# The last block of a relational graph layer, multiplied in two halves with upper and lower parts in one stationary

## The chip, the cores and the metric

The kernel runs on one core of a Trainium2 chip. The metric is the device time in microseconds (us); the number shown is the median of three runs.

## What is computed

A relational graph layer with a residual and a layer norm. There are 6250 nodes with 256 features, 206250 edges sorted by destination, and 16 relations with a 256 x 256 weight each:

```python
transformed = jnp.einsum('ni,rio->rno', h, weight)
msg = transformed[rel_type, src] * norm
out = jax.ops.segment_sum(msg, dst, num_segments=h.shape[0])
x = _layernorm(x + out, axis=-1)
```

## The kernel before

The kernel sums first and multiplies afterwards. Nodes go in blocks of 128 (SB); there are 49 blocks (NB), and the last one has 106 nodes (LAST). A block has four parts (groups) of 32 nodes (GN). For each part, edges come in tiles of 128. GpSimd gathers the source rows of a tile with an indirect DMA (L557) into `rows`. VectorE makes the tile's spread matrix (L786): one column for each pair of node and relation in the tile's window, the edge's weight where it belongs. TensorE multiplies the rows by the spread into PSUM `ps_a` (L983); this adds, for each node and relation, the weighted source rows, and is called A. Each step has two k-halves of 128 features, and the trace shows four matmuls a step (float32, two each).

When a part has all its tiles, ScalarE copies A out of PSUM with rounding (L857, the upper part `a_hi`, float32r), and VectorE subtracts this from PSUM to get what is left (L752, the lower part `a_lo`). Upper and lower weights lie side by side in `w_parts`. The products of a block are 32 k-tiles (16 relations x 2 halves). For each, the upper A of 128 nodes is the stationary against upper and lower weights, 512 columns (L942), and the lower A is the stationary against the upper weights, 256 columns (L944). They add up in one bank of `ps_z`. `normalise` (L725 to L743) on VectorE adds the node's own row and both halves of the bank, makes mean and variance, waits for ScalarE's square root (L881), and writes the normalised rows, which SP stores (L522).

The order is written out by hand. Each engine runs through the same list of blocks and steps (`blocks`, L416), and the engines are held together by semaphores only. At step t of block b, TensorE does the sums of the step and then some products of block b-1, from step 8 on (`products_at`, L178). In the last block (39 steps, 0 to 38) these are two k-tiles a step at steps 8 to 23. After the last block come two rounds of 40 steps without sums: the first holds the products of the last block (from step 8 on, with nothing between), the second its normalisation. `normalise(b)` handles block b-2 and stands at step 10 (NORM_AT) of round b; block 47 is thus normalised in the round behind the sums.

Evacuation lags behind the sums: ScalarE copies a part 4 steps after it closes (EVAC_LAG), VectorE subtracts 9 steps after (LOWER_LAG), counted in each engine's own list. In the last block, part 192 (group 0) closes at step 11, part 193 at step 22, part 194 at step 33, part 195 (10 nodes) at step 38. So VectorE's subtractions for part 193 stand in its list at step 31, behind that step's spread. The spreads have 17 slots, so VectorE can be 17 steps ahead of TensorE. The spreads of steps 23 to 38 have 96, 160, 208, 208, 224, 224, 240, 192, 144, 80, 96, 96, 160, 128, 64 and 16 columns.

SP's list has, for each block, the edge loads, and then the wait for that block's normalisation, the store of its rows, and the load of the next own rows into `xr`. At the end it waits for the last normalisation, and stores 96 and 10 rows (L525 to L528).

Of the kernel before, what the change touches and what calls it, by code (L numbers as in the profile page):

```python
# [87 lines left out]
def build(nc, x, src, dst, rel, norm, weight, out):  # L88
# [86 lines left out]
    NORM_AT = 10  # L175
    ENDED_AT, TOTAL_STEP, FLAG_AT = 12, 14, 18

    def products_at(b, t):  # L178
        if b == NB - 1:
            return 2 if PRODUCT_FROM <= t < PRODUCT_FROM + KH * R // 2 else 0  # L180

        def upto(t):
            return 0 if t < PRODUCT_FROM else ceil(KH * R * (t - PRODUCT_FROM + 1) / (length[b] - PRODUCT_FROM))
        return upto(t) - upto(t - 1)
# [15 lines left out]
    with ExitStack() as ctx:  # L200
# [114 lines left out]
        def spread_at(n):  # L315
# [5 lines left out]
                return over_below[:, later * WMAX:later * WMAX + WMAX]  # L321
            return over_w_raw[:, (later - fit) * WMAX:(later - fit) * WMAX + WMAX]

        hit_cmp = z_rows.rearrange("p n f -> p (n f)")[:, 0:2 * SROW].rearrange("p (q e) -> p q e", q=2)

        ps_f = ps_m[:, 256:512]
# [55 lines left out]
        a_upper_made = sem("a_upper_made")  # L382
        products_made = sem("products_made")
        own_rows_in = sem("own_rows_in")
        residual_added = sem("residual_added")
        upper_added = sem("upper_added")
        variance_steps = sem("variance_steps")
# [37 lines left out]
        def prepared(b, t, step):  # L425

            if b == 0:
                return [1] if t == FIRST_PREPARE[step] else []
            found = [2] if b == 1 and t == SECOND_PREPARE[step] else []
            if t == PREPARE[step] and 3 <= b + AHEAD < NB:  # L430
                found.append(b + AHEAD)
            return found

        evacuated_at = {}
        for part, n in closes.items():
# [36 lines left out]
        def fast_sync(sp):  # L472
            def load_edges(b):

                for s in range(GROUPS):
                    n = GROUPS * (b - 1) + s
                    first = sp.value_load(first_i[0:1, n:n + 1], min_val=0, max_val=E)
                    sp.dma_start(raw[PT * s:PT * s + PT, :, :],
                                 packed[:, bass.ds(first, PART_EDGES)].rearrange("a (j p) -> j a p", p=P)).then_inc(
                                     edges_in, 16)  # L480

            def raw_left(b):

                sp.wait_ge(edges_converted, b)
                sp.wait_ge(edges_turned, b)

            def load_weights(n):
                if n >= 2:

                    sp.wait_ge(w_lower_made, n - 1)  # L490
                sp.dma_start(w_raw[:, n % 2, :, :], weight[n, :, :].rearrange("(k p) n -> p k n", p=P)).then_inc(
                    weights_in[n % 2], 16)

            sp.dma_start(direct_idx[:, :], src[0:DIRECT * P].rearrange("(j p) -> p j", p=P),
                         allow_slow_non_contiguous=True).then_inc(direct_idx_in, 16)
            for a, v in enumerate((src, dst, rel, norm_i)):
                sp.dma_start(raw[0:CT, a, :], v[0:CE].rearrange("(j p) -> j p", p=P)).then_inc(edges_in, 16)

            sp.dma_start(sample_i[0:SP, :], dst.rearrange("(p c e) -> p c e", c=SC, e=SROW)[:, :, 0],
                         allow_slow_non_contiguous=True).then_inc(samples_in, 16)  # L500
            sp.dma_start(xr[:, :], x[0:SB, :]).then_inc(own_rows_in, 16)
            for n in range(WEIGHTS_BEFORE):
                load_weights(n)

            sp.wait_ge(first_edges_ready, 1)
            sp.wait_ge(edges_packed, 8 * 16)
            raw_left(1)
            load_edges(1)
            for n in range(WEIGHTS_BEFORE, R):
                load_weights(n)  # L510
            raw_left(2)
            load_edges(2)
            raw_left(3)
            load_edges(3)
            for b in range(1, NB):
                if b + 3 < NB:
                    raw_left(b + 3)
                    load_edges(b + 3)

                sp.wait_ge(rows_normalised, b)  # L520
                rows_of = min(SB, N - b * SB)
                sp.dma_start(out[(b - 1) * SB:b * SB, :], z_out[:, :]).then_inc(rows_out, 16)  # L522
                sp.dma_start(xr[0:rows_of, :], x[b * SB:b * SB + rows_of, :]).then_inc(own_rows_in, 16)

            sp.wait_ge(rows_normalised, NB)  # L525
            EVEN = LAST // 16 * 16
            sp.dma_start(out[(NB - 1) * SB:N - LAST + EVEN, :], z_out[0:EVEN, :]).then_inc(rows_out, 16)
            sp.dma_start(out[N - LAST + EVEN:N, :], z_out[EVEN:LAST, :]).then_inc(rows_out, 16)  # L528
            flag = uncounted(sp)
            sp.wait_ge(rows_out, (NB + 1) * 16)  # L530
            return flag

        def fast_pool(pool):
# [78 lines left out]
        def fast_vector(dve):  # L612
# [112 lines left out]
            def normalise(b):  # L725
# [16 lines left out]
                dve.tensor_scalar(z_out[:, :], z[:, :], z_mv[:, 0:1], z_rstd[:, :],  # L742
                                  ALU.subtract, ALU.mult).then_inc(rows_normalised, 1)  # L743

            def lower_part(part):
                b, g = part // GROUPS, part % GROUPS
                for h in range(KH):

                    dve.wait_ge(a_upper_made, KH * part + h + 1)
                    nodes = min(GN, N - GN * part)  # L750
                    at_g = slice(g * GN, g * GN + nodes)
                    dve.tensor_tensor(a_lo[:, b % 2, h, :, at_g],  # L752
                                      ps_a[:, g % OPEN, h, 0:nodes * R].rearrange("p (n r) -> p r n", r=R),
                                      a_hi[:, b % 2, h, :, at_g].bitcast(F32), ALU.subtract).then_inc(
                                          a_lower_made, 1)

            def tile_block(b, sums, products, rows_):
                for t in range(length[b]):
# [30 lines left out]
                                          ALU.is_equal, ALU.mult).then_inc(spreads_made, 1)  # L789
                    for part in evacuated_at.get(n - LOWER_LAG, ()):  # L790
                        lower_part(part)
                    if rows_ and t == NORM_AT:
                        normalise(b)

            first_runs = runs([step.first * R for step in plan[0]])
            for base, t0, t1 in first_runs:
# [12 lines left out]
            seek_samples()  # L809
            seek = {SEEK_ROW: seek_row, SEEK_EDGE: seek_edge, SEEK_TABLE: seek_table, SEEK_COPY: seek_copy}  # L810
            blocks(dve, tile_block)


        def runs(values):
# [4 lines left out]
        def fast_scalar(act):  # L819
# [27 lines left out]
            def evacuate(part):  # L847
                b, g = part // GROUPS, part % GROUPS


                act.wait_ge(tiles_summed, signals(closes[part]))
                if g == 0:

                    wait(act, products_made, b, 1, -1)
                nodes = min(GN, N - GN * part)
                for h in range(KH):
                    act.activation(a_hi[:, b % 2, h, :, g * GN:g * GN + nodes],  # L857
                                   ps_a[:, g % OPEN, h, 0:nodes * R].rearrange("p (n r) -> p r n", r=R),
                                   ACT.Copy).then_inc(a_upper_made, 1)

            def tile_block(b, sums, products, rows_):
                for t in range(length[b]):
                    if sums:
                        if b == 0 and t in WEIGHTS_AT:
                            n = WEIGHTS_AT[t]

                            act.wait_ge(weights_in[n % 2], 16 * (n // 2 + 1))
                            act.activation(w_parts[:, n, :, 0, :], w_raw[:, n % 2, :, :], ACT.Copy).then_inc(
                                w_upper_made, 1)
                        for ahead in prepared(b, t, CONVERT):  # L870
                            convert_edges(ahead)
                        for ahead in prepared(b, t, COPY):
                            copy_edges(ahead)
                    for part in evacuated_at.get(start_of[b] + t - EVAC_LAG, ()):
                        evacuate(part)
                    if rows_ and t == NORM_AT:
                        if b == 2:

                            act.wait_ge(columns_made, 2)
                        wait(act, variance_steps, b, 2, -2)  # L880
                        act.activation(z_std[:, :], z_mv[:, 1:2], ACT.Sqrt, bias=eps_col[:, :]).then_inc(  # L881
                            deviation_made, 1)

            convert_edges(0)
            copy_edges(0)
            pack_edges()
            blocks(act, tile_block)

        def fast_tensor(pe):
            def seek_count():  # L890
# [38 lines left out]
            def product(b, n):  # L929
# [16 lines left out]
                if n == KH * R - 1:  # L946
                    ins.then_inc(products_made, 1)

            def tile_block(b, sums, products, rows_):
                done, arrived = 0, set()  # L950
                for t in range(length[b]):
                    if sums:
# [34 lines left out]
                                    start=opens[part] == n, stop=False, skip_group_check=True)  # L987
                        if n in ends:
                            ins.then_inc(tiles_summed, 1)
                    if products:  # L990
                        for _ in range(products_at(b, t)):
                            product(b, done)
                            done += 1


            pe.wait_ge(constants_made, 4)
# [216 lines left out]
```

## Time and profile before

| | |
|---|---|
| median of three runs | 2483.79 us (2480.95 to 2488.75) |
| span of the profiled execution | 2053.3 us |
| its own whole time | not given beside its span |
| TensorE (PE) busy | 1949.3 us, 95% |
| GpSimd (POOL) busy | 1536.3 us, 75% |
| VectorE (DVE) busy | 1264.7 us, 62% |
| ScalarE (ACT) busy | 272.9 us, 13% |
| mean granted clock of TensorE | 0.993 |

The span goes from the first to the last instruction of one profiled execution. PE is TensorE's matmul, PEld its weight load, which overlaps. Matmul ends are modelled: matmuls are pipelined, so the distance between two starts is what one costs, not its duration. The chain of waits follows the last instruction back to what released each step. PEclk is the clock granted to TensorE, 1.00 being 2.4 GHz and 0.50 being 1.2 GHz.

### The profile page before, as it was taken

The numbers are of one execution on the slowest core, as the hardware profiler recorded it, in microseconds if no ns is written. First come the engines' busy times: TensorE is split into PE (matmuls) and PEld (weight loads), VectorE is DVE, ScalarE is ACT, GpSimd is POOL, SyncE is SP. The second block draws the span as 40 slices with busy tenths as digits, with TensorE's granted clock in tenths as the row PEclk, the third lists the DMA queues.
The fourth block names the chain that finished last, engine by engine and source line by source line (L and its number), as shares of the span: only waits on it lengthen the run. The fifth ranks groups of instructions, "written<-read, shape, count | busy, mean of one in ns | idle before, by whom it ended". The sixth has DMA issues, their size and how long they took to land. (4 is left out here: it accounts for less than half of the span.)

```text
span 2053.3 us, 33711 instructions
## 1 busy us (share of the span) xinstructions
PE 1949.3 (95%) x11962; PEld 1813.6 (88%) x11962; DVE 1264.7 (62%) x3579; ACT 272.9 (13%) x557; POOL 1536.3 (75%) x1649
## 2 busy tenths in 40 slices
PE   5899999999999999999999999999999999999998
PEld 4799999998889888998898898888898889988887
DVE  5666666666666666666566656666665656566554
ACT  1211111111111111111111111111111111111110
POOL 7777777777777777777777777777777777777774
PEclk8999999999999999999999999999999999999999
DMA  6544334344444444434344434344433434444332
GB/s 205 150 113 118 114 113 118 114 113 113 118 114 113 113 118 113 114 113 118 113 114 113 117 113 114 112 115 116 114 113 113 119 113 113 113 117 114 112 111 76
DMA packets 107715, 239.00 MB, mean 116 GB/s; under 512 B 31226, under 2 KB 55642, under 8 KB 107482
## 3 DMA queue, kind: packets, MB, share of 16 engines
q0 software_dynamic: 77760, 212.43, 36.6%
q1 hardware_dynamic: 29342, 21.02, 3.5%
q10 hardware_dynamic: 440, 3.32, 0.4%
q8 instruction: 99, 1.62, 0.4%
q14 instruction: 74, 0.61, 0.1%
HBM read 230.23 MB, written 9.72 MB: 117 GB/s over the span
## 5 line engine op out<-in xcount | busy, mean ns | idle before, releaser
L557 POOL DMA_INDIRECT rows<-in_x,idx x1614 | 1528.1, 947 | 491.7 <-issue 330.6
L983 PE MATMUL ps_a<-spread,rows 128*128 128x96 f32 (+7 forms) x5700 | 1066.0, 320 | 61.3 <-DMA rows<-in_x,idx 33.3
L983 PEld LDWEIGHTS ps_a<-spread,rows 128*128 128x128 f32 x5700 | 877.8, 192 | 137.5 <-DVE spread L786 40.7
L942 PE MATMUL ps_z<-w_parts,a_hi 128*128 128x512 f32 x1568 | 803.9, 514 | 1.0 <-DVE a_lo L752 1.0
L752 DVE TENSOR_TENSOR a_lo<-ps_a,a_hi 128x512 fp32r<-128x512 f32 x392 | 251.2, 683 | 487.7 <-ACT a_hi L857 487.7
L786 DVE TENSOR_SCALAR spread<-ps_i,key,meta 128x96 f32<-128x96 f32 (+8 forms) x1415 | 542.4, 449 | 5.5 <-PE ps_a L983 5.5
L944 PE MATMUL ps_z<-w_parts,a_lo 128*128 128x256 f32 x1568 | 439.7, 280 | 0.0
L857 ACT ACTIVATE a_hi<-ps_a 128x512 fp32r<-128x512 f32 x392 | 212.3, 594 | 1230.8 <-PE ps_a L983 1230.8
L942 PEld LDWEIGHTS ps_z<-w_parts,a_hi 128*128 128x128 f32 x1568 | 298.7, 190 | 5.0 <-DVE a_lo L752 1.1
L944 PEld LDWEIGHTS ps_z<-w_parts,a_lo 128*128 128x128 f32 x1568 | 299.1, 191 | 1.8
L983 PE MATMUL ps_a<-w_raw,rows 128*128 128x208 f32 (+7 forms) x1452 | 273.8, 318 | 14.7 <-DMA rows<-in_x,idx 13.2
L983 PE MATMUL ps_a<-below,rows 128*128 128x224 f32 (+7 forms) x1452 | 274.1, 318 | 12.3 <-DMA rows<-in_x,idx 9.9
L983 PEld LDWEIGHTS ps_a<-w_raw,rows 128*128 128x128 f32 x1452 | 222.5, 190 | 34.9 <-DVE spread L786 11.2
L983 PEld LDWEIGHTS ps_a<-below,rows 128*128 128x128 f32 x1452 | 222.5, 190 | 32.7 <-DVE spread L786 9.8
L786 DVE TENSOR_SCALAR below<-ps_i,key,meta 128x96 f32<-128x96 f32 (+7 forms) x363 | 144.9, 448 | 0.0
L786 DVE TENSOR_SCALAR w_raw<-ps_i,key,meta 128x208 f32<-128x208 f32 (+7 forms) x363 | 144.7, 448 | 0.0
L702 DVE CAST idx<-meta 128x40 int32<-128x40 f32 x48 | 14.1, 294 | 203.5 <-ACT meta L835 203.5
L835 ACT ACTIVATE meta<-ps_m 128x160 f32<-128x160 f32 (+1 forms) x49 | 14.8, 303 | 375.9 <-PE ps_m L926 375.9
L720 DVE SCALAR_TENSOR_TENSOR key<-tile_no,tiles_of,key_all 128x10 f32<-128x10 f32 x192 | 44.3, 231 | 6.9
L881 ACT ACTIVATE z_std<-z_mv,eps_col 128x1 f32<-128x1 f32 x49 | 14.4, 295 | 132.8 <-DVE z_mv L736 132.8
L926 PEld LDWEIGHTS ps_m<-ident,raw_f 40*128 40x128 f32 (+1 forms) x147 | 13.0, 141 | 18.1 <-issue 17.1
L826 ACT ACTIVATE raw_f<-raw 40x384 f32<-40x384 int32 (+1 forms) x49 | 25.1, 512 | 7.2 <-DMA raw<-packed 4.8
(75 smaller groups left out, 263.5 us busy)
## 6 DMA issues: line engine op xcount, KB each, us to landing
rows<-in_x,idx POOLq DMA_INDIRECT x1614, 2.8
xr<-in_x SPq DMA_DIRECT2D x48, 128.0 KB
out<-z_rows SPq DMA_DIRECT2D x48, 128.0 KB
w_raw<-in_L_gnn_weight SPq DMA_DIRECT2D x16, 256.0 KB, 3.1
raw<-packed SPq DMA_DIRECT2D x192, 20.0 KB
packed<-in_src ACTq DMA_DIRECT2D x1, 805.7 KB, 6.0
packed<-in_dst ACTq DMA_DIRECT2D x1, 805.7 KB, 7.6
packed<-in_edge_type ACTq DMA_DIRECT2D x1, 805.7 KB, 9.1
```

What stands on the lines that cost most here:

```text
L557: pool.indirect_dma_start(rows[:, row, :], None, x, bass.IndirectOffsetOnAxis(ap=index, axis=0)).then_inc(arrived, 16)
L702: dve.tensor_copy(idx[:, k, :], m[:, 0, :]).then_inc(keys_made, 1)
L720: key_done(dve.scalar_tensor_tensor(out=key[:, k, PT * s:PT * s + PT], in0=tile_no[:, :], scalar=tiles_of[:, n:n + 1], in1=key_all[:, PT * ...
L752: dve.tensor_tensor(a_lo[:, b % 2, h, :, at_g], ps_a[:, g % OPEN, h, 0:nodes * R].rearrange("p (n r) -> p r n", r=R), a_hi[:, b % 2, h, :, ...
L786: dve.tensor_scalar(spread_at(n)[:, 0:width], iota[:, 0:width], key[:, b % SLOTS, step.column:step.column + 1], meta[:, b % SLOTS, 3, step ...
L826: act.activation(raw_f[0:C, :, :], raw[0:C, 0:3, :], ACT.Copy).then_inc(edges_converted, 1)
L835: act.activation(meta[:, k, :, 0:C], ps_m[:, 0:4 * C].rearrange("p (a t) -> p a t", a=4), ACT.Copy).then_inc(edges_copied, 1)
L857: act.activation(a_hi[:, b % 2, h, :, g * GN:g * GN + nodes], ps_a[:, g % OPEN, h, 0:nodes * R].rearrange("p (n r) -> p r n", r=R), ACT.Co ...
L881: act.activation(z_std[:, :], z_mv[:, 1:2], ACT.Sqrt, bias=eps_col[:, :]).then_inc(deviation_made, 1)
L942: pe.matmul(zk, a_hi[:, ak, h, r, :], w_parts[:, r, h, :, :].rearrange("p a f -> p (a f)"), start=n == 0, stop=False, skip_group_check=True)
L944: ins = pe.matmul(zk[:, 0:F], a_lo[:, ak, h, r, :], w_parts[:, r, h, 0, :], start=False, stop=n == KH * R - 1, skip_group_check=True)
L983: ins = pe.matmul(ps_a[:, g % OPEN, h, (begin - zero) * R:(stop - zero) * R], rows[:, step.row, h * P:(h + 1) * P], spread_at(n)[:, (begin ...
```

## The change

The last block's 106 nodes are multiplied in halves of 64 and 42 nodes. Groups 0 and 1 put their upper A into columns 0 to 63 and their lower A into columns 64 to 127 of the same `a_hi` buffer; groups 2 and 3 do the same in `a_lo`. One matmul of 512 columns a k-tile gives rows 0 to 63 (upper A by both weights) and rows 64 to 127 (lower A by both weights). The first half's products go in TensorE's list behind the sums of steps 27 to 37 of the last block, three a step; the second half's stand behind all sums. ScalarE copies the lower rows' first 256 columns down to the partitions of the upper rows, and VectorE adds own rows, both column halves and this copy before the statistics. Each half has its own store; the second half's own rows have a load of their own. The normalisation of block 47 moves to step 28 of the last block. The buffers are existing ones.

```diff
+    HALF_ROWS = (64, LAST - 64)
+    HALF_FROM, HALF_EACH, LAST_NORM_AT = 27, 3, 28
...
+        half_sum = (ps_z[:, (NB - 1) % 2, :], ps_m[:, :])
+        half_own = (xr, col_iota[:, 0:F])
...
+        def upper_at(part, h, nodes):
+            b, g = part // GROUPS, part % GROUPS
+            if b == NB - 1:
+                return (a_hi, a_lo)[g // 2][:, b % 2, h, :, GN * (g % 2):GN * (g % 2) + nodes]
+            return a_hi[:, b % 2, h, :, g * GN:g * GN + nodes]
+
+        def lower_at(part, h, nodes):
+            b, g = part // GROUPS, part % GROUPS
+            if b == NB - 1:
+                return (a_hi, a_lo)[g // 2][:, b % 2, h, :, 64 + GN * (g % 2):64 + GN * (g % 2) + nodes]
+            return a_lo[:, b % 2, h, :, g * GN:g * GN + nodes]
...
-            sp.wait_ge(rows_normalised, NB)
-            EVEN = LAST // 16 * 16
-            sp.dma_start(out[(NB - 1) * SB:N - LAST + EVEN, :], z_out[0:EVEN, :]).then_inc(rows_out, 16)
-            sp.dma_start(out[N - LAST + EVEN:N, :], z_out[EVEN:LAST, :]).then_inc(rows_out, 16)
+            sp.wait_ge(columns_made, 3)
+            late = N - HALF_ROWS[1]
+            sp.dma_start(half_own[1][0:HALF_ROWS[1], :], x[late:N, :]).then_inc(late_own_rows_in, 16)
+
+            sp.wait_ge(half_normalised, 1)
+            sp.dma_start(out[late - HALF_ROWS[0]:late, :], half_out[0][0:HALF_ROWS[0], :]).then_inc(rows_out, 16)
+            sp.wait_ge(half_normalised, 2)
+            EVEN = HALF_ROWS[1] // 16 * 16
+            sp.dma_start(out[late:late + EVEN, :], half_out[1][0:EVEN, :]).then_inc(rows_out, 16)
+            sp.dma_start(out[late + EVEN:N, :], half_out[1][EVEN:HALF_ROWS[1], :]).then_inc(rows_out, 16)
...
+            def normalise_half(n):
+                S, sums, step = slice(0, HALF_ROWS[n]), half_sum[n], count(6 * n + 1)
...
+                dve.wait_ge(half_products_made, n + 1)
+                dve.wait_ge(half_lower_moved, n + 1)
...
+                step_done(dve.tensor_tensor(half_one[n][S, :], half_own[n][S, :], sums[S, 0:F], ALU.add))
+                step_done(dve.tensor_tensor(half_two[n][S, :], half_one[n][S, :], sums[S, F:2 * F], ALU.add))
+                step_done(dve.tensor_tensor(half_one[n][S, :], half_two[n][S, :], half_low[n][S, :], ALU.add))
+                step_done(dve.bn_stats(z_stat[S, :], half_one[n][S, :]))
+                step_done(dve.bn_aggr(z_mv[S, :], z_stat[S, :]))
+                dve.wait_ge(half_deviation_made, n + 1)
+                step_done(dve.reciprocal(z_rstd[S, :], z_std[S, :]))
+                dve.tensor_scalar(half_out[n][S, :], half_one[n][S, :], z_mv[S, 0:1], z_rstd[S, :],
+                                  ALU.subtract, ALU.mult).then_inc(half_normalised, 1)
...
-                    if rows_ and t == NORM_AT:
+                    if rows_ and t == NORM_AT and b < NB:
                         normalise(b)
+                    if b == NB - 1 and t == LAST_NORM_AT:
+                        normalise(NB)
...
             blocks(dve, tile_block)
+            for n in range(2):
+                normalise_half(n)
...
+            def half_lower(n):
+
+                act.wait_ge(half_products_made, n + 1)
+                act.activation(half_low[n][0:HALF_ROWS[n], :], half_sum[n][64:64 + HALF_ROWS[n], 0:F],
+                               ACT.Copy).then_inc(half_lower_moved, 1)
...
+            def half_product(g, n):
+
+                r, h = n // KH, n % KH
+                if n == 0:
+                    pe.wait_ge(a_lower_made, (PARTS - GROUPS + 2 * g + 2) * KH)
+                    if g == 0:
+                        pe.wait_ge(residual_added, NB - 2)
+                    else:
+                        pe.wait_ge(flag_steps, 2)
+                        pe.wait_ge(edges_copied, NB)
+                ins = pe.matmul(half_sum[g], (a_hi, a_lo)[g][:, (NB - 1) % 2, h, r, :],
+                                w_parts[:, r, h, :, :].rearrange("p a f -> p (a f)"),
+                                start=n == 0, stop=n == KH * R - 1)
+                if n == KH * R - 1:
+                    ins.then_inc(half_products_made, 1)
...
-                    if products:
+                    if products and b < NB:
...
+                    if b == NB - 1 and t >= HALF_FROM:
+                        for n in range(HALF_EACH * (t - HALF_FROM), HALF_EACH * (t - HALF_FROM + 1)):
+                            if n < KH * R:
+                                half_product(0, n)
+                    if b == NB and t == 0:
+                        for n in range(KH * R):
+                            half_product(1, n)
```

ScalarE's step 10 for block 47 (the square root) moves to its step 28 in the same way, and after its list come, for each half, the copy and the square root.

## Rows read from the trace of the kernel before

**Rows 1.** The page: span, and TensorE's busy time.

```profile
span 2053.3 us, 33711 instructions
PE 1949.3 (95%) x11962; PEld 1813.6 (88%) x11962; DVE 1264.7 (62%) x3579; ACT 272.9 (13%) x557; POOL 1536.3 (75%) x1649
```

**Rows 2.** The gathers' line: duration ns min/median/max, first and last start; landing.

```profile
L557 POOL DMA_INDIRECT rows<-in_x,idx x1614: 942/946/1427, 8.5 to 2030.1; - x180
...
DMA to landing us min/median/max: 2.6/2.8/11.0
```

**Rows 3.** Waits over the span: us in total, times, longest.

```profile
PE ps_a L983 <- DMA rows<-in_x,idx: 56.4, 92, 1.6
```

**Rows 4.** Busy time in stretches (length, PE, PEld, DVE, ACT, POOL; clock; DMA).

```profile
2006.90:2026.96 20.06, 20.06 (x128) 18.63 (x128) 8.77 (x21) 2.17 (x4) 15.18 (x17) 1.00 0.41 114
2026.96:2035.50 8.54, 8.54 (x60) 8.39 (x59) 3.34 (x10) 1.09 (x2) 3.21 (x4) 1.00 0.31 75
2036.48:2048.06 11.58, 11.56 (x64) 9.80 (x64) 1.88 (x6) 0.29 (x1) 0.00 (x0) 1.00 0.07 22
```

**Rows 5.** Chain of waits in the last block: start, us, what.

```profile
2012.53 0.54 PE ps_a L983 x4
...
2015.17 0.70 PE ps_a L983 x4
...
2016.57 0.76 PE ps_a L983 x4
...
2023.93 0.27 PE ps_z L942
...
2026.96 8.55 PE ps_a L983 x60
```

**Rows 6.** Timeline of VectorE in the last block.

```profile
2014.52 1.36 DVE L786 TENSOR_SCALAR below<-ps_i,key,meta 128x224 f32<-128x224 f32 x3
2015.79 0.81 DVE L786 TENSOR_SCALAR w_raw<-ps_i,key,meta 128x192 f32<-128x192 f32 x2
2025.75 1.29 DVE L752 TENSOR_TENSOR a_lo<-ps_a,a_hi 128x512 fp32r<-128x512 f32 x2 [9.15 <-ACT a_hi L857]
...
2036.34 0.41 DVE L730 TENSOR_TENSOR z_rows<-xr,ps_z 128x256 f32<-128x256 f32 x1
```

**Rows 7.** Chain of waits behind the sums: start, us, what.

```profile
2036.48 0.50 PE ps_z L942
...
2037.10 0.23 PE ps_z L942
...
2047.93 0.13 PE ps_z L944
...
2048.09 0.43 DVE z_rows L730
...
2050.20 0.41 DVE z_rows L742
```

**Rows 8.** Timeline of SP: the last two stores.

```profile
2050.64 0.34 SPq L527 DMA_DIRECT2D out<-z_rows  x1
2051.03 0.36 SPq L528 DMA_DIRECT2D out<-z_rows  x1
```

**Rows 9.** Stretches around falls of the clock (columns as in rows 4).

```profile
57.89:60.15 2.26, 0.00 (x0) 0.00 (x0) 0.88 (x2) 0.63 (x1) 1.73 (x2) 1.00 0.76 250
...
63.47:66.98 3.51, 3.51 (x13) 3.47 (x14) 3.24 (x6) 0.63 (x1) 2.78 (x3) 0.50 0.74 232
...
2048.06:2050.10 2.04, 0.00 (x0) 0.00 (x0) 1.55 (x5) 0.29 (x1) 0.00 (x0) 1.00 0.00 0
2050.10:2053.30 3.20, 0.00 (x0) 0.00 (x0) 0.47 (x2) 0.00 (x0) 0.00 (x0) 0.50 0.13 37
```

**Rows 10.** ScalarE's evacuations from 2020 us on, by shape.

```profile
L857 ACT ACTIVATE a_hi<-ps_a 128x512 fp32r<-128x512 f32 x4 | 2.2, 595 | 20.4 <-PE ps_a L983 20.4
...
L857 ACT ACTIVATE a_hi<-ps_a 128x160 fp32r<-128x160 f32 x2 | 0.5, 302 | 1.2 <-PE ps_a L983 1.2
```

More of the change, by code:

```diff
@@ L176, in build @@
     ENDED_AT, TOTAL_STEP, FLAG_AT = 12, 14, 18
+    HALF_ROWS = (64, LAST - 64)
+    HALF_FROM, HALF_EACH, LAST_NORM_AT = 27, 3, 28
+    assert 64 == 2 * GN and NB % 2 and length[NB - 1] > HALF_FROM + KH * R // HALF_EACH
     def products_at(b, t):
@@ L322, in spread_at @@
             return over_w_raw[:, (later - fit) * WMAX:(later - fit) * WMAX + WMAX]
+        half_sum = (ps_z[:, (NB - 1) % 2, :], ps_m[:, :])
+        half_own = (xr, col_iota[:, 0:F])
+        half_low = (spread[:, 0, 0:F], spread[:, 1, 0:F])
+        half_one = (z_rows[:, 1, :], spread[:, 2, 0:F])
+        half_two = (z_rows[:, 0, :], spread[:, 3, 0:F])
+        half_out = (z_rows[:, 2, :], spread[:, 4, 0:F])
         hit_cmp = z_rows.rearrange("p n f -> p (n f)")[:, 0:2 * SROW].rearrange("p (q e) -> p q e", q=2)
@@ L384, in build @@
         own_rows_in = sem("own_rows_in")
+        late_own_rows_in = sem("late_own_rows_in")
+        half_products_made = sem("half_products_made")
+        half_lower_moved = sem("half_lower_moved")
+        half_steps = sem("half_steps")
+        half_deviation_made = sem("half_deviation_made")
+        half_normalised = sem("half_normalised")
         residual_added = sem("residual_added")
@@ L523, in fast_sync @@
                 sp.dma_start(xr[0:rows_of, :], x[b * SB:b * SB + rows_of, :]).then_inc(own_rows_in, 16)
-            sp.wait_ge(rows_normalised, NB)
-            EVEN = LAST // 16 * 16
-            sp.dma_start(out[(NB - 1) * SB:N - LAST + EVEN, :], z_out[0:EVEN, :]).then_inc(rows_out, 16)
-            sp.dma_start(out[N - LAST + EVEN:N, :], z_out[EVEN:LAST, :]).then_inc(rows_out, 16)
+            sp.wait_ge(columns_made, 3)
[7 more added lines that the diff above has]
+            sp.dma_start(out[late + EVEN:N, :], half_out[1][EVEN:HALF_ROWS[1], :]).then_inc(rows_out, 16)
             flag = uncounted(sp)
-            sp.wait_ge(rows_out, (NB + 1) * 16)
+            sp.wait_ge(rows_out, (NB + 2) * 16)
             return flag
@@ L743, in normalise, with step_done @@
                                   ALU.subtract, ALU.mult).then_inc(rows_normalised, 1)
+            def normalise_half(n):
+                S, sums, step = slice(0, HALF_ROWS[n]), half_sum[n], count(6 * n + 1)
+                def step_done(ins):
+                    ins.then_inc(half_steps, 1)
+                    dve.wait_ge(half_steps, next(step))
+                dve.wait_ge(half_products_made, n + 1)
+                dve.wait_ge(half_lower_moved, n + 1)
+                if n == 0:
+                    dve.wait_ge(own_rows_in, NB * 16)
+                    dve.wait_ge(rows_out, (NB - 1) * 16)
+                else:
+                    dve.wait_ge(late_own_rows_in, 16)
+                step_done(dve.tensor_tensor(half_one[n][S, :], half_own[n][S, :], sums[S, 0:F], ALU.add))
[7 more added lines that the diff above has]
+                                  ALU.subtract, ALU.mult).then_inc(half_normalised, 1)
             def lower_part(part):
@@ L750, in lower_part @@
                     nodes = min(GN, N - GN * part)
-                    at_g = slice(g * GN, g * GN + nodes)
-                    dve.tensor_tensor(a_lo[:, b % 2, h, :, at_g],
+                    dve.tensor_tensor(lower_at(part, h, nodes),
                                       ps_a[:, g % OPEN, h, 0:nodes * R].rearrange("p (n r) -> p r n", r=R),
-                                      a_hi[:, b % 2, h, :, at_g].bitcast(F32), ALU.subtract).then_inc(
+                                      upper_at(part, h, nodes).bitcast(F32), ALU.subtract).then_inc(
                                           a_lower_made, 1)
@@ L856, in evacuate, with deviation, half_deviation @@
                 for h in range(KH):
-                    act.activation(a_hi[:, b % 2, h, :, g * GN:g * GN + nodes],
+                    act.activation(upper_at(part, h, nodes),
                                    ps_a[:, g % OPEN, h, 0:nodes * R].rearrange("p (n r) -> p r n", r=R),
                                    ACT.Copy).then_inc(a_upper_made, 1)
+            def deviation(b):
+                wait(act, variance_steps, b, 2, -2)
+                act.activation(z_std[:, :], z_mv[:, 1:2], ACT.Sqrt, bias=eps_col[:, :]).then_inc(deviation_made, 1)
+            def half_lower(n):
+                act.wait_ge(half_products_made, n + 1)
+                act.activation(half_low[n][0:HALF_ROWS[n], :], half_sum[n][64:64 + HALF_ROWS[n], 0:F],
+                               ACT.Copy).then_inc(half_lower_moved, 1)
+            def half_deviation(n):
+                act.wait_ge(half_steps, 6 * n + 5)
+                S = slice(0, HALF_ROWS[n])
+                act.activation(z_std[S, :], z_mv[S, 1:2], ACT.Sqrt, bias=eps_col[S, :]).then_inc(
+                    half_deviation_made, 1)
             def tile_block(b, sums, products, rows_):
@@ L875, in tile_block @@
                         evacuate(part)
-                    if rows_ and t == NORM_AT:
+                    if rows_ and t == NORM_AT and b < NB:
                         if b == 2:
                             act.wait_ge(columns_made, 2)
-                        wait(act, variance_steps, b, 2, -2)
-                        act.activation(z_std[:, :], z_mv[:, 1:2], ACT.Sqrt, bias=eps_col[:, :]).then_inc(
-                            deviation_made, 1)
+                        deviation(b)
+                    if b == NB - 1 and t == LAST_NORM_AT:
+                        deviation(NB)
             convert_edges(0)
@@ L887, in fast_scalar @@
             blocks(act, tile_block)
+            for n in range(2):
+                half_lower(n)
+                half_deviation(n)
         def fast_tensor(pe):
@@ L947, in product @@
                     ins.then_inc(products_made, 1)
+            def half_product(g, n):
+                r, h = n // KH, n % KH
+                if n == 0:
+                    pe.wait_ge(a_lower_made, (PARTS - GROUPS + 2 * g + 2) * KH)
+                    if g == 0:
+                        pe.wait_ge(residual_added, NB - 2)
+                    else:
+                        pe.wait_ge(flag_steps, 2)
[5 more added lines that the diff above has]
+                    ins.then_inc(half_products_made, 1)
             def tile_block(b, sums, products, rows_):
```

## The prediction, made before the result was known

> **What bounds the kernel now.** I read the page first, then the gathers, then the waits, then the last block by stretches, and last the chain of waits from its end backwards. Over the whole span TensorE is busy 95% [rows 1], but the page warns that this is modelled, so it proves nothing. The gathers tell more: 1614 of them run from 8.5 to 2030.1 us, which is 1.25 us for each, 0.95 us of work and 0.3 us of issue, with next to nothing between [rows 2]. TensorE's waits for a gather come to 56 us in 92 waits, the longest of 1.6 us [rows 3]. So in the long run the gathers set the pace and TensorE follows closely behind them. None of that is changed here. The change is in the last 45 us, and there the order is another. From 2006.90 to 2026.96 TensorE is busy 20.06 of 20.06 us, from there to 2035.50 busy 8.54 of 8.54 us [rows 4]. In the first of these stretches it does steps 8 to 23 of the last block with two k-tiles of products of block 47 behind each; in the second it does steps 24 to 38, sums only, at 8.54 / 15 = 0.57 us a step. It has fallen behind the gathers and catches up. The last gather is issued at 2030.1 and lands 2.8 us behind its issue (median) [rows 2], about 2033.9 with its own 0.95 us, 1.6 us before the sums end. **There is no hole in TensorE's work at steps 27 to 37 that new work could fill.** Behind the sums stand 0.98 us for the last part's evacuation, 11.58 us of products for block 48 (2036.48 to 2048.06), 2.55 us of normalisation and 2.7 us of stores [rows 4, 7, 8].
>
> The profiled execution has a span of 2053.3 us [rows 1]; its own whole time is not given beside it. The median of the runs is 2483.79 us, so 430.5 us lie around the span. I take them as fixed, since nothing in the trace shows them, and set my sum, a difference, on the median.
>
> **1. The tail's products, made shorter.** Before: 32 k-tiles, each a 512-column and a 256-column matmul, 0.235 + 0.119 us, 11.58 us in all [rows 4, 7]. After: the second half (42 nodes) takes 32 matmuls of 512 columns. The stationary is still 128 columns and the moving operand the same 512, so the price is the row of the same instruction: 32 x 0.235 = 7.5 us, plus 0.26 us because the first one behind a wait takes 0.50 and not 0.24 us [rows 7]. 7.78 in place of 11.58: **-3.8 us**. One weight load per matmul (0.19 us each, under 0.235) stays hidden. The rows price a matmul by its moving columns (0.235 against 0.119 us for half of them), and the nodes are on the stationary side, so I take no gain for fewer nodes; that is why two halves cost 64 x 0.235 = 15.0 us together where the whole block cost 11.3.
>
> To weigh: the Trainium skill (TensorE: Matmul & The Clock Gate, section Back-to-back issue gap) gives some 131 ns for a 512-column matmul in a stream of pairs with weight loads; by that figure the sum of this whole text would be about 7 us less, close to no change. This trace has the same instruction in the same surroundings at 235 ns, and I go by it.
>
> **2. The first half, moved into the loop.** 32 matmuls of 512 columns stand three a step behind the sums of steps 27 to 36, two behind step 37. 32 x 0.235 = 7.5, and 0.03 us more for the first behind narrow sums (0.27 against 0.23 [rows 5, 7]), some six times: 7.7 us. Since TensorE has no idle time there [rows 4], all of it lies on the path: **+7.7 us**. If gathers had paced this stretch the price would be 0; the rows exclude that for this execution.
>
> **3. The normalisation of block 47, moved from behind all sums to step 28 of the last block.** Before it ran at 2036.34 [rows 6], beside the products, at no cost. Now it stands in VectorE's queue behind the spread of step 28, and ahead of the spreads of steps 29 to 31 and of the lower parts of group 1. VectorE runs far ahead: it makes the spreads of 27 to 29 at 2014.52 and of 30 and 31 at 2015.79, then waits [rows 6]. After the change it will stop at about 2015.5 for the last product of block 47, which TensorE ends at 2026.96 [rows 5]. From there: normalisation 2.52 us (2048.09 to 2050.61 [rows 7]), to 2029.5; spreads of 29, 30, 31, by the starts in [rows 6] about 0.45 + 0.75 us, to 2030.7; two subtractions 1.29 us [rows 6], to 2032.0. These subtractions used to be done at 2027.04. And the first product of the half waits for them (parts 192 and 193, both k-halves). TensorE reaches that wait after steps 24 to 27, 0.54 + 0.70 + 0.70 + 0.76 = 2.70 us by steps of the same widths [rows 5], at 2029.66. It stands until 2032.05, a wait of 2.4 us, plus 0.26 us for the start behind a wait: **+2.65 us**. Bounds: 0, if the subtractions were ahead of the normalisation after all; 3.5, if semaphores and the square root on ScalarE take more than in the tail. Behind this wait stand all later sums; nothing else is late. The spreads 32 to 38 need only earlier steps of TensorE, ScalarE's next evacuation is due after step 33, and the two transfers that SP issues after this normalisation (rows out, own rows in) come ten microseconds earlier than before. They fall beside the last two gathers, which now have over 7 us to spare.
>
> **4. TensorE's clock.** The wait of part 3 is longer than any that TensorE has for a gather [rows 3]. The granted clock fell to 0.50 after a stretch of 2.26 us without work at 57.9 us, and after 2.04 us at the very end; once work was back at 63.47 it stayed at half for 3.51 us more [rows 9]. That would cost 3.51 / 2 = 1.75 us. Bounds: 0 (the clock holds) and 3.5 (half speed for twice as long). The rows that fell had as long an idle time as mine, so I count half of 1.75: **+0.9 us**. The Trainium skill (TensorE: Matmul & The Clock Gate, section HAM oscillation — how this bites in real kernels) says that waits between bursts throw the engine back to half rate; it speaks against this change, and these rows agree with it.
>
> **5. The end.** ScalarE first copies the lower rows' 256 columns out of PSUM, and VectorE waits for it: 160 columns take 0.30, 512 take 0.595 us [rows 10], so 0.38 + 0.03 for the hop. Then one more addition, 0.45 us [rows 7]. For VectorE's work on 42 rows in place of 128 no row has a price; it could save up to 1 us if time went by rows, and I take none, since the columns stay at 256. The stores: 32 + 10 rows in place of 96 + 10, two issues of 0.35 us as before [rows 8], the last one as small as before; gain between 0 and 0.3 us, I take 0. The half of 64 rows is normalised and stored while TensorE does the 7.8 us of the second, 3 us of work beside 7.8. **+0.85 us**.
>
> **Sum:** -3.8 + 7.7 + 2.65 + 0.9 + 0.85 = **+8.3 us**, 2492.1 us. The other waits and the two small loads (late own rows, issued early) cost nothing: they are met long before. About 0.3% (7.5 us) is what a measurement of this kernel can tell from no change, and my sum is just above it.
>
> **Rivals.**
> - **The gathers pace the last block in the timed runs** (ends not slower). 430 us outside the span are unexplained; if they are gathers slower by 0.27 us each (430 / 1614), a gather takes 1.5 us. Then the products behind a step (0.7) and its sums (0.57) fit under it, parts 2 to 4 vanish under waits, and -3.8 + 0.85 = -2.95 us remains: 2480.8. For: 1.25 us a gather is the long-run pace [rows 2]. Against: the stretches with no wait [rows 4]. It decides from 1.3 us a gather on.
> - **VectorE does not hold TensorE up** (the change's own order works as written, "steps 27 to 37"): -3.8 + 7.7 + 0.85 = +4.75 us, 2488.5. For: VectorE was 10 us ahead. Against: the queue order of part 3. Also the case in which the change does only in part what it says: the products begin at 27 but late.
> - **The clock falls for long**: 3.5 in place of 0.9, and a wait of 3.5 in place of 2.65: +11.8 us, 2495.5. For: [rows 9]. Against: the work before and after the wait is dense.
>
> **How the numbers follow.** Forecast 0.63, own range 2490.5 to 2494; gathers 0.13; no hold-up 0.13; long fall 0.11. The forecast lies close to the bound, and a measured median of this kernel moves by a few microseconds (2480.95 to 2488.75 in three runs), so of its 0.63 I give 0.41 to slower and 0.22 to within 0.3%. The long fall is slower (0.11). No hold-up is within (0.12) but for 0.01 slower. The gathers' case is within (0.08) or faster (0.05), a little more for what I overlook. Together: faster 0.06, within 0.41, slower 0.53. The range runs from 2484 to 2496: it takes in the no-hold-up case and the long fall, and leaves the gathers' case out.
>
> **What would show it.** In the profile after: 32 matmuls of 512 columns at 0.235 us behind the sums, last product about 7.8 us behind the last evacuation; a wait of TensorE for the lower parts (the subtractions) of 2.4 us at step 27; the normalisation of block 47 right behind its last product; the sums' end about 10 us later than 2035.5; the granted clock about 1.00, or half for some microseconds behind the wait; a span near 2060.7. Wrong if TensorE waits for gathers between steps 28 and 38, if its wait at step 27 is under 1 us, or if a 512-column matmul of the halves takes other than 0.235 us.

## The result, and the profile after

The changed kernel takes 2491.40 us (median of 14 runs, 2486.73 to 2493.23), the kernel before 2482.51 us (14 runs). The ratio is 1.0028, with a 95% interval of 1.0019 to 1.0037. It is slower by 0.28%, 7.0 us by the ratio and 8.9 us by the medians. Forecast were 2492.1 us and +8.3 us.

The page of the changed kernel, span and TensorE:

```profile
span 2490.3 us, 33728 instructions
PE 2129.6 (86%) x11962; PEld 1908.5 (77%) x11962; DVE 1269.3 (51%) x3587; ACT 274.4 (11%) x560; POOL 1540.0 (62%) x1649
```

This execution's own time is 2492.0 us, so 1.7 us lie around its span. The span is 437 us longer than that of the first profile [rows 1], of which the change explains 8; that difference is taken up under the first experiment. The end of the work compares directly. TensorE in the last block (timeline: start, us, engine, line, operation; in brackets the idle time before):

```profile
2455.02 0.40 PE L1023 MATMUL ps_z<-w_parts,a_hi 128*128 128x512 f32 x1
2455.26 0.28 PE L1025 MATMUL ps_z<-w_parts,a_lo 128*128 128x256 f32 x1
2455.38 2.11 PE L1080 MATMUL ps_a<-spread,rows 128*128 128x160 f32 x12
2457.32 0.92 PE L1080 MATMUL ps_a<-below,rows 128*128 128x224 f32 x4
2460.51 0.96 PE L1040 MATMUL ps_z<-w_parts,a_hi 128*128 128x512 f32 x3 [2.26 <-DVE a_hi L810]
2461.31 1.20 PE L1080 MATMUL ps_a<-below,rows 128*128 128x224 f32 x4
2462.00 1.79 PE L1040 MATMUL ps_z<-w_parts,a_hi 128*128 128x512 f32 x3
2463.59 1.78 PE L1080 MATMUL ps_a<-below,rows 128*128 128x240 f32 x4
...
2466.43 0.99 PE L1040 MATMUL ps_z<-w_parts,a_hi 128*128 128x512 f32 x3
...
2476.66 7.56 PE L1040 MATMUL ps_m<-w_parts,a_lo 128*128 128x512 f32 x32 [0.98 <-DVE a_lo L810]
```

The last product of block 47 ends at 2455.54. Steps 24 to 27 follow; then TensorE stands for 2.26 us in front of the first half's first product. The three products at 2462.00 and the step behind them then take 1.59 and 1.27 us from start to start, about twice the 0.86 and 0.63 us that the same work takes in experiment 2. The second half is one block of 7.56 us where [rows 4] has 11.58. VectorE meanwhile:

```profile
2455.57 0.42 DVE L765 TENSOR_TENSOR z_rows<-xr,ps_z 128x256 f32<-128x256 f32 x1 [10.72 <-PE ps_z L1025]
...
2457.69 0.41 DVE L777 TENSOR_SCALAR z_rows<-z_rows,z_mv,z_rstd 128x256 f32<-128x256 f32 x1
2458.02 0.52 DVE L844 TENSOR_SCALAR below<-ps_i,key,meta 128x240 f32<-128x240 f32 x1
2458.45 0.81 DVE L844 TENSOR_SCALAR w_raw<-ps_i,key,meta 128x192 f32<-128x192 f32 x2
2459.18 1.28 DVE L810 TENSOR_TENSOR a_hi<-ps_a,a_hi 128x512 fp32r<-128x512 f32 x2
```

It waits 10.72 us for block 47's last product, with all that stands behind it: normalisation, three spreads, and then the two subtractions for which TensorE waits. Before, the same subtractions stood ahead of the normalisation [rows 6]. The clock, in stretches of the changed kernel (columns as in [rows 4]):

```profile
2458.16:2460.51 2.35, 0.09 (x2) 0.00 (x1) 2.35 (x6) 0.00 (x0) 0.00 (x0) 1.00 0.28 77
...
2461.31:2461.70 0.39, 0.39 (x4) 0.39 (x3) 0.39 (x2) 0.00 (x0) 0.00 (x0) 1.00 0.12 37
2461.70:2461.90 0.20, 0.20 (x2) 0.20 (x1) 0.20 (x2) 0.00 (x0) 0.00 (x0) 0.77 0.14 51
...
2462.01:2465.43 3.42, 3.42 (x10) 2.83 (x9) 0.41 (x2) 0.00 (x0) 0.00 (x0) 0.53 0.05 16
2465.43:2475.70 10.27, 10.24 (x62) 9.03 (x60) 1.29 (x2) 1.09 (x2) 0.00 (x0) 1.00 0.00 0
```

The clock fell to its half level between 2461.7 and 2461.9, 1.3 us after the wait had ended, while TensorE was busy again, and stayed there for 3.4 us. (The stretch from 2462.01 to 2465.43 begins 0.2 us behind the fall and ends 0.2 us behind the rise, hence its mean of 0.53.) The end, in the chain of waits:

```profile
2484.25 0.39 ACT spread L930
2484.72 0.42 DVE spread L794
2485.17 0.42 DVE spread L795
2485.62 0.43 DVE spread L796
```

These are the copy by ScalarE and three additions, where before there were two.

### The profile page after: what moved, and what is told of

The parts are those of the page before. It is cut to its first block, busy times and chain, and to the rows that moved or that the text cites. A ratio compares the mean times of both kernels' runs of the same rounds, so it can differ in the third digit from the quotient of the medians.

```text
span 2490.3 us, 33728 instructions
## 1 busy us (share of the span) xinstructions
PE 2129.6 (86%) x11962; PEld 1908.5 (77%) x11962; DVE 1269.3 (51%) x3587; ACT 274.4 (11%) x560; POOL 1540.0 (62%) x1649
## 4 chain that ended last, share of the span: by engine, by line
PE 64%; issue 17%; DVE 10%; another core or an unknown queue 6%; ACT 2%; DMA 1%; SPq 1%; ACTq 0%; DVEq 0%
PE ps_a L1080 44%; PE ps_z L1023 13%; PE ps_z L1025 6%; DVE spread L844 3%; DVE a_lo L810 3%; ACT a_hi L919 1%; DVE below L844 1%; DVE w_raw L844 1%; PE ps_m L1007 1%; DMA packed<-pad_i 0%; PE ps_z L1040 0%; DVE z_rows L777 0%; DVE z_stat L769 0%; DVE z_rows L767 0%
## 5 line engine op out<-in xcount | busy, mean ns | idle before, releaser
L1080 PE MATMUL ps_a<-spread,rows 128*128 128x96 f32 (+7 forms) x5700 | 1126.7, 328 | 177.0 <-issue 137.5
L1080 PEld LDWEIGHTS ps_a<-spread,rows 128*128 128x128 f32 x5700 | 915.7, 198 | 275.0 <-issue 177.4
L1023 PE MATMUL ps_z<-w_parts,a_hi 128*128 128x512 f32 x1536 | 818.8, 534 | 64.5 <-issue 40.2
L1025 PE MATMUL ps_z<-w_parts,a_lo 128*128 128x256 f32 x1536 | 449.0, 292 | 31.1 <-issue 31.0
L1023 PEld LDWEIGHTS ps_z<-w_parts,a_hi 128*128 128x128 f32 x1536 | 308.4, 201 | 95.2 <-issue 61.5
L1080 PE MATMUL ps_a<-below,rows 128*128 128x224 f32 (+7 forms) x1452 | 301.1, 333 | 37.2 <-issue 33.2
L1080 PE MATMUL ps_a<-w_raw,rows 128*128 128x208 f32 (+7 forms) x1452 | 288.9, 326 | 24.0 <-issue 22.7
L1080 PEld LDWEIGHTS ps_a<-below,rows 128*128 128x128 f32 x1452 | 239.9, 203 | 61.4 <-issue 41.3
L1080 PEld LDWEIGHTS ps_a<-w_raw,rows 128*128 128x128 f32 x1452 | 233.6, 198 | 50.7 <-issue 35.4
L1007 PE MATMUL ps_m<-ident,raw_f 40*128 40x40 f32 (+1 forms) x147 | 19.9, 247 | 11.2 <-issue 6.5
```

Source lines behind the costliest of these rows:

```text
L1007: ins = pe.transpose(ps_m[:, a * C:(a + 1) * C], v, ident[0:C, 0:C])
L1023: pe.matmul(zk, a_hi[:, ak, h, r, :], w_parts[:, r, h, :, :].rearrange("p a f -> p (a f)"), start=n == 0, stop=False, skip_group_check=True)
L1025: ins = pe.matmul(zk[:, 0:F], a_lo[:, ak, h, r, :], w_parts[:, r, h, 0, :], start=False, stop=n == KH * R - 1, skip_group_check=True)
L1080: ins = pe.matmul(ps_a[:, g % OPEN, h, (begin - zero) * R:(stop - zero) * R], rows[:, step.row, h * P:(h + 1) * P], spread_at(n)[:, (begin ...
```

## The experiments

Experiments 1 to 4 ran on one chip, 5 to 8 on another; each ratio is to runs of the kernel before on the same chip. Each execution's end is measured from one point, the end of block 47's last product. "Sums" is from there to the first evacuation of the last part, "products" from there to the last matmul, "rest" to the end of the span, all in us:

| kernel | sums | products | rest | total |
|---|---|---|---|---|
| before, first profile | 8.58 | 12.51 | 5.25 | 26.3 |
| before, second profile | 8.58 | 12.51 | 5.27 | 26.4 |
| changed, first profile | 20.17 | 8.51 | 6.08 | 34.8 |
| changed, second profile | 20.13 | 8.52 | 6.01 | 34.7 |
| normalisation at step 32 | 15.98 | 8.51 | 6.04 | 30.5 |
| first half at steps 30 to 37 | 16.31 | 8.50 | 6.10 | 30.9 |
| both halves behind the sums | 8.67 | 14.61 | 6.05 | 29.3 |
| before, with the wait alone | 11.11 | 12.52 | 5.24 | 28.9 |
| step 32, first half twice | 23.36 | 8.52 | 6.05 | 37.9 |

**1. The kernel before, a second profile.** No edit.

> The kernel before, unchanged, for a second profile. Theory: the change touches only the last block, so the 430 us between the span of the first profile (2053.3 us) and the median (2483.8 us) have nothing to do with it, and the last block looks as in the first profile: TensorE without a wait from step 8 to step 38, 0.98 us of wait, 11.58 us of products, 5.24 us to the end. Rival (gathers pace the last block in ordinary executions): waits of TensorE for gathers in steps 24 to 38, together 3 us or more.

The last block is the same to 0.02 us, and TensorE has no wait in it until the 0.98 us behind the sums:

```profile
2497.78 1.30 PE L983 MATMUL ps_a<-spread,rows 128*128 128x128 f32 x11
2500.07 0.50 PE L942 MATMUL ps_z<-w_parts,a_hi 128*128 128x512 f32 x1 [0.98 <-DVE a_lo L752]
```

But the span is 2516.9 us at a time of 2518.57 us (this run was on another chip, where the kernel before has a median of 2520.88). So the first profile was of an unusually short execution, and almost nothing lies around a span. TensorE's waits over the whole span:

```profile
PE ps_a L983 <- issue: 183.2, 307, 5.5
PE ps_a L983 <- DVE spread L786: 43.4, 17, 17.8
PE ps_z L942 <- issue: 42.9, 64, 1.7
...
PE ps_z L944 <- issue: 24.4, 47, 1.5
...
PE ps_m L926 <- issue: 17.7, 19, 1.8
```

In place of 56 us of waits for gathers [rows 3] there are 268 us of waits called "issue", for nothing that the profile shows; the first profile lists none of them for TensorE. GpSimd is ahead here, and in the line of the gathers it waits for TensorE:

```profile
L557 POOL DMA_INDIRECT rows<-in_x,idx x1614: 941/948/1278, 8.5 to 2465.3; - x180
its engine sat idle before it (us, times) until:
  PE ps_a L983: 422.7, 372
```

The last gather is issued at 2465.3, 34 us ahead of the sums' end. Gathers do not pace the last block; TensorE does.

**2. The normalisation at step 32.**

```diff
-    HALF_FROM, HALF_EACH, LAST_NORM_AT = 27, 3, 28
+    HALF_FROM, HALF_EACH, LAST_NORM_AT = 27, 3, 32
```

> The change, with the normalisation of block 47 at step 32 in place of 28, behind the subtractions for part 193. Theory (TensorE's wait of 2.3 us at step 27 and the half clock behind it come from VectorE's order): the wait is gone, the clock stays, the sums end 3.5 to 4 us earlier relative to the last product of block 47 (20.2 us in the changed kernel, 16.4 expected = 8.54 + 7.8), and the time is 4 us below the changed kernel, 0.18% above the kernel before. Rival (the wait comes from the subtractions' own lateness, wherever the normalisation stands): the wait stays at 2 us or more and the time stays 0.28% above. Rival (the products would be hidden if the wait were gone): back to the kernel before or faster, 0.1% below.

Ratio to the kernel before 1.0020 (1.0011 to 1.0030). TensorE runs through:

```profile
2489.46 0.92 PE L1080 MATMUL ps_a<-below,rows 128*128 128x224 f32 x4
2490.05 1.02 PE L1040 MATMUL ps_z<-w_parts,a_hi 128*128 128x512 f32 x3
2490.91 0.92 PE L1080 MATMUL ps_a<-below,rows 128*128 128x224 f32 x4
```

No wait until the 0.98 us behind the sums, no fall of the clock, 4.2 us less than the changed kernel. The products in the loop cost 15.98 - 8.58 = 7.4 us, all of it exposed. The interval alone would not separate this from the changed kernel; the trace does.

**3. The first half at steps 30 to 37.**

```diff
-    HALF_FROM, HALF_EACH, LAST_NORM_AT = 27, 3, 28
+    HALF_FROM, HALF_EACH, LAST_NORM_AT = 30, 4, 28
```

> The change, with the normalisation left at step 28 and the first half's products at steps 30 to 37, four a step. Theory: TensorE reaches the wait 2.4 us of sums later (steps 28 to 30), when the subtractions are just done; a wait under 0.5 us is left, the clock stays, and the time is as in the variant with the normalisation at step 32, 0.15 to 0.2% above the kernel before. Rival (the subtractions' place does not matter): time as the changed kernel, 0.28% above.

Ratio 1.0024 (1.0014 to 1.0034); 16.31 us, no wait listed and no fall. The same hold-up removed from the other side: the consumer comes later. A trace of it is left:

```profile
2491.53 1.28 DVE L810 TENSOR_TENSOR a_hi<-ps_a,a_hi 128x512 fp32r<-128x512 f32 x2
...
2492.00 0.81 PE L1080 MATMUL ps_a<-w_raw,rows 128*128 128x192 f32 x4
2492.86 1.19 PE L1040 MATMUL ps_z<-w_parts,a_hi 128*128 128x512 f32 x4
```

The subtractions end at 2492.81, and the first product starts 0.86 us behind the start of its step's sums, where the same pair is 0.52 us apart in experiment 2. Because matmul ends are modelled, no idle time is listed for this; it is the 0.3 us by which the loop is longer than there.

**4. Both halves behind the sums.**

```diff
-                    if b == NB - 1 and t >= HALF_FROM:
...
-                                half_product(0, n)
                     if b == NB and t == 0:
+                        for n in range(KH * R):
+                            half_product(0, n)
...
```

> The change, with the first half's 32 products taken out of steps 27 to 37 and put behind all sums, ahead of the second half's. Theory (TensorE has no idle time in the loop, so the place of the 7.5 us is the same to it): block of 64 matmuls of 0.235 us = 15.0 us behind the sums, no wait at step 27, total +3.5 (products) + 0.85 (end) + 0.0 = 4.3 us above the kernel before, 0.17%, the same as the variant with the normalisation at step 32. Rival (part of the 7.5 us is hidden in the loop): slower than that variant by what was hidden, up to 7.5 us, 0.3%.

Ratio 1.0015 (1.0002 to 1.0027). It is not equal to experiment 2 but 1.2 us shorter (29.3 against 30.5): the first half's products need nothing of the last part, so they start at once behind the sums and cover the evacuation of the last part.

```profile
2501.15 7.54 PE L1040 MATMUL ps_z<-w_parts,a_hi 128*128 128x512 f32 x32
2508.54 7.41 PE L1040 MATMUL ps_m<-w_parts,a_lo 128*128 128x512 f32 x32
```

So nothing had been hidden in the loop; putting them there even left the one real hole, behind the sums, unused. I had not expected that.

**5. The kernel before, with the wait alone.** ScalarE's square root for block 47 moves to its step 28 as well; that part of the edit is left out here.

```diff
...
+                    if b == NB - 1 and t == 28:
+                        normalise(NB)
...
+                        if b == NB - 1 and t == 27:
+                            pe.wait_ge(a_lower_made, (PARTS - GROUPS + 2) * KH)
```

> The kernel before, with two things of the change alone: block 47's normalisation at step 28 of the last block, and TensorE waiting behind the sums of step 27 for the subtractions of part 193. No product is moved or reshaped. Theory: the wait alone is 2.3 us and 0.26 us at its restart; from block 47's last product to the end 26.36 + 2.3 to 2.6 = 28.7 to 29.0 us if the clock holds, up to 1.7 us more if it falls; the time is 0.1 to 0.17% above the kernel before. Rival (the order of VectorE's work is harmless and the moved products alone cost the changed kernel's 8.4 us): 26.4 us, no change.

```profile
2466.50 1.83 PE L989 MATMUL ps_a<-below,rows 128*128 128x224 f32 x8 [2.27 <-DVE a_lo L752]
2473.59 0.50 PE L948 MATMUL ps_z<-w_parts,a_hi 128*128 128x512 f32 x1 [0.99 <-DVE a_lo L752]
```

The clock behind the wait (columns as in [rows 4]):

```profile
2466.50:2472.60 6.10, 6.10 (x44) 5.96 (x44) 3.20 (x9) 1.09 (x2) 0.00 (x0) 1.00 0.06 20
```

A wait of 2.27 us, 2.53 us in all; the clock stayed at 1.00 this time. Ratio 1.0011 (1.0001 to 1.0021), as expected.

**6. The first half's products twice**, with the normalisation at step 32. Only the second pass signals that they are done.

```diff
...
-                        for n in range(HALF_EACH * (t - HALF_FROM), HALF_EACH * (t - HALF_FROM + 1)):
-                            if n < KH * R:
-                                half_product(0, n)
+                        for n in range(2 * HALF_EACH * (t - HALF_FROM), 2 * HALF_EACH * (t - HALF_FROM + 1)):
+                            if n < 2 * KH * R:
+                                half_product(0, n % (KH * R), n >= KH * R)
```

> The variant with the normalisation at step 32, with the first half's 32 matmuls of steps 27 to 37 done twice (six a step, the second time over from the start). Theory (nothing there is hidden): 32 x 0.235 = 7.5 us more than that variant, 30.53 + 7.5 = 38.0 us from block 47's last product to the end, time 0.5% above the kernel before. Rival (part of the first 7.5 us had been hidden under gathers or issue): the second pass costs more than the first one's 7.4 us, or, were there still room, less than 7 us.

37.9 us, 7.4 us more than with one pass; ratio 1.0045 (1.0029 to 1.0060). The second pass costs what the first one did.

**7. The changed kernel, a second profile.** No edit.

> The changed kernel once more, for a second profile. Theory: the wait of TensorE at step 27 is 2.26 us again, since it comes from the order of work; whether the clock falls behind it differs from execution to execution. From block 47's last product to the end 33.1 us if the clock holds and 34.8 us if it falls as in the first profile. Rival (the fall belongs to the wait as such): 34.7 us or more again.

```profile
2465.52 1.22 PE L1040 MATMUL ps_z<-w_parts,a_hi 128*128 128x512 f32 x3 [2.27 <-DVE a_hi L810]
```

```profile
2465.98:2469.40 3.42, 3.42 (x11) 2.82 (x10) 1.45 (x6) 0.00 (x0) 0.00 (x0) 0.51 0.09 30
```

The wait is the same, and the clock fell again for 3.4 us, this time 0.5 us after the wait had ended. With experiment 5 that is two falls behind three waits of the same length.

**8. Three k-tiles of block 47 kept for the hole behind the sums**, in the kernel before.

```diff
+    KEPT = 3
...
-            return 2 if PRODUCT_FROM <= t < PRODUCT_FROM + KH * R // 2 else 0
+            return max(0, min(2, KH * R - KEPT - 2 * (t - PRODUCT_FROM))) if PRODUCT_FROM <= t < PRODUCT_FROM + KH * R // 2 else 0
...
+                    if b == NB and t == 0:
+                        for n in range(KH * R - KEPT, KH * R):
+                            product(NB - 1, n)
```

> The kernel before, with the last 3 of block 47's 32 k-tiles kept back from steps 22 and 23 and done behind the sums of step 38, where TensorE stands for 0.98 us. Theory: they are 3 x 0.354 = 1.06 us of work that fills the wait; from the sums' end to the last product 12.51 us become 11.5 plus at most 0.1, the sums end 1.06 us earlier, and from the end of block 47's 29th k-tile to the end 1.0 to 1.25 us are gained; the time 0.05% below the kernel before, under what can be measured in the total. Rival (block 47's normalisation, now later, holds something up): equal or slower by up to 1 us.

```profile
2461.78 0.48 PE L943 MATMUL ps_z<-w_parts,a_hi 128*128 128x512 f32 x1
...
2462.80 0.28 PE L945 MATMUL ps_z<-w_parts,a_lo 128*128 128x256 f32 x1
2462.92 0.49 PE L943 MATMUL ps_z<-w_parts,a_hi 128*128 128x512 f32 x1
```

The three kept k-tiles run from 2461.78 to the second line, and the last block's first product follows at once: the hole is gone. From the end of block 47's 29th k-tile to the end of the span it takes 26.66 us, in both profiles of the kernel before 27.84 and 27.86: a gain of 1.2 us (the 0.98 us, and the slow start of the first product behind a wait). Ratio 0.9994 (0.9983 to 1.0004), so the total does not show it. No version here is measurably faster than the kernel before.

## Why the prediction was right

The sum was +8.3 us; the profiles give 34.76 - 26.34 = 8.4 us. The mechanism is the one foretold: no idle time in the loop, a hold-up by VectorE's order, a shorter tail that does not pay for it. Term by term:

- **Part 1, the tail's products.** Forecast -3.8, measured 8.51 - 12.51 = -4.0 us, with the wait ahead of them unchanged. The matmul of 512 columns costs 0.235 us in both halves (7.4 to 7.6 us for 32). That the halves have 64 and 42 nodes tests nothing, since the stationary side keeps its 128 columns in both.
- **Part 2, the first half in the loop.** Forecast +7.7, measured +7.4 (experiments 2 and 6). That TensorE had no idle time there was the decisive reading.
- **Part 3, the hold-up by VectorE's order.** Forecast +2.65 (a wait of 2.4), measured +2.53 (a wait of 2.26 to 2.27; experiment 5 alone, experiments 2 and 3 by taking it away).
- **Part 4, the clock.** Forecast +0.9, half the price of a fall; what is left of the changed kernel's 11.59 us in the loop, 11.59 - 7.40 - 2.53 = 1.7 us, is the whole price, forecast at 1.75. The same comes out directly: from the start of step 28's sums to the first evacuation of the last part it takes 14.40 us, and 12.74 us in experiment 2, where the clock held. It fell in both profiles of the changed kernel, not in experiment 5.
- **Part 5, the end.** Forecast +0.85, measured 6.08 - 5.25 = +0.8 us. Fewer rows gave nothing: an addition of 256 columns takes VectorE 0.41 us with 42 and with 64 rows and 0.42 us with 128.

**Where it was luck.** That the sum is right to 0.1 us is luck. Part 4 was 0.8 us too small, and parts 1 to 3 together 0.6 us too large. Half the price of a fall is a mean of two cases and could not come out in any one execution: the same parts give +6.7 where the clock holds and +8.4 where it falls.

**What it had wrong**, none of which moved the sum by much:

- It took 430 us for time around the span, and foretold a span near 2060.7 us. They are inside ordinary spans: the changed kernel's is 2490.3 us.
- "In the long run the gathers set the pace" held for the first profile alone; in the other profile of the kernel before GpSimd waits for TensorE. The two agree on the last block to 0.02 us all the same, and that block carried the argument.
- Its reason for a fall of the clock, that "the rows that fell had as long an idle time as mine", misreads those rows. At 57.9 us the clock fell when 2.26 us without work had passed, but the wait went on to 5.58 us (the line below, from the kernel before), and at the end of the span TensorE had no more work at all. Neither row showed what a wait of 2.3 us does once it is over.
- Its aside that a cheaper 512-column matmul would take some 7 us off the sum counts only the kernel after. The kernel before has 32 of the same matmuls in its own tail, so about half of that would go. With 0.235 us measured it plays no part.

```profile
63.47 8.74 PE L983 MATMUL ps_a<-spread,rows 128*128 128x208 f32 x41 [5.58 <-DVE a_lo L752]
```

The rival of the gathers falls with experiments 1 and 6; in the changed kernel TensorE has no wait for a gather from 2436 us to the end, and the last gather is issued at 2430.17, 45 us ahead of the sums' end. The rival without a hold-up falls with experiment 5 and the waits in the traces; the total alone does not exclude it, since its +4.75 us is just inside the interval of the ratio (4.7 to 9.2 us). The rival of the long fall was not seen: both falls lasted 3.4 us. Nor can the interval separate the case with a hold-up and a fall (+8.4) from the one with a hold-up alone (+6.7).

## What to carry to other kernels

Before work is moved out of a tail, look whether the engine has idle time at the place where it goes. Here a split that shortened the tail by 4 us raised the engine's work on these products from 11.6 to 15.0 us and put the extra where every microsecond counted. When a long piece of work is moved ahead in an engine's list, count what stands behind it there and who waits for that: 2.5 us of normalisation moved past two subtractions cost 2.5 us on another engine, and the cheap cure was four places later in the list. The one real hole (0.98 us behind the sums) can be filled: by the first half (experiment 4), and better by three k-tiles that have to be done anyway (experiment 8).

## What the runs showed of the hardware

- One profiled execution need not stand for the timed ones. The first profile of the kernel before has a span of 2053.3 us, where its timed runs took 2480.95 to 2488.75 us; the second has 2516.9 us in a run of 2518.57 us (on a chip whose median is 1.5% higher). In the long one TensorE waited 268 us for nothing that the profile shows and had a mean granted clock of 0.938, against none of these waits and 0.993. What makes these waits is open; no run here tried it.
- A wait of 2.3 us inside dense work was followed by half clock for 3.4 us in two of three profiles. The fall came after the wait had ended, 1.3 us behind it in one and 0.5 us in the other. Why it did not come in the third is open.
